# Graph aggregation of a four-layer graph network in 64x64 tiles of the PE array, with re-paired batches and two output banks

## The chip, the cores and the metric

The kernel runs on one core of one Trainium2 chip. The metric is the device time of that core in microseconds (us); less is better. Of the kernel before there are three timed runs: 1529.56, 1530.80 and 1532.76 us, median 1530.8 us.

## The reference, cut to what matters

A batch of 128 graphs, each with 64 nodes and 256 features in fp32, passes through four residual layers that share one 64x64 adjacency matrix. Layers 0 and 1 are masked multi-head attention, layer 2 is graph attention, and layer 3 is a gated recurrence of three steps. The change touches layer 2 alone:

```
h = maximum(layernorm(x), 0)          # [128, 64, 256]
hw = h @ W                            # [128, 64, 256]
e = leaky_relu(hw @ a1 [:, :, None] + hw @ a2 [:, None, :], 0.2) * adj
att = softmax(e, axis=2)              # [128, 64, 64], one matrix for each graph
x = x + elu(att @ hw + beta * hw)
```

So `att @ hw` is, for each of 128 graphs, a product of a 64x64 matrix with a 64x256 matrix.

## The kernel before, in words

**Tiling.** `x` stays in SBUF for the whole run, as 64 tiles of 128 partitions by 256 features. A tile holds two graphs, one on partitions 0 to 63 and one on 64 to 127. Work goes in chunks of `CT` = 4 tiles (eight graphs), so there are 16 chunks. PSUM is eight banks: four are named `scores` (in the later part also `high`), four `ring`.

**Stages.** Layers 0 and 1 run as one pipeline over 32 chunk steps and take about the first 600 us. Then comes a stage in which layers 2 and 3 are interleaved: `halves` issues 49 half steps of the recurrence, six for a group of two chunks, and layer 2 of the next group's chunks is put between them. Each half step has attributes that say what it carries. Where `graph_a` is set (half steps 1 and 3 of a group), TensorE transposes the normalised rows of a chunk (`graph_rows`, line 1536) and multiplies them by `W` (`graph_product`); ScalarE copies the result into `hw`; `graph_s2` makes the second score term. Where `graph_b` is set (half steps 2 and 4), TensorE transposes the attention matrices (`graph_attT`), VectorE adds beta times the identity and writes `attT` (`copy_attT`), and TensorE makes the aggregation (`graph_aggregate`, line 1558). Layer 2 of chunks 0 and 1 runs ahead of that: chunk 0's aggregation in the last steps of layer 1, into `scores`; chunk 1's in `begin`, into `ring`, from `hw_next`.

**The aggregation before.** `attT[:, t, :]` is a 128x128 block-diagonal matrix with the transposed attention of the two graphs of tile `t`. It is the stationary operand; the moving operand is `hw[:, t, 0:256]`. One matmul for each tile, four for a chunk, each shown in the trace as two instructions (fp32 goes through the array twice). Tiles 0 and 1 fill bank `bank`, tiles 2 and 3 bank `bank + 1`; after two tiles `y_ready` goes up.

**Who reads it.** ScalarE reads each bank once (`graph_read`, line 805: minus the negative part, into `y_neg`), then takes an exponential (line 810). VectorE adds the positive part of each bank to `x` (`graph_positive`, line 1199) and then the exponential (line 1210). In a half step that carries an aggregation TensorE's order is: eight transposes, `u3` (12 matmuls of 512 columns), `adjacency` (line 1579), `u5` (12), transposes of the attention (line 1556), `w4` (12), the aggregation, `w3` (12), `w5` (12). These products all go through the helper at line 99. VectorE's order is r_sum (1249), the low parts (1301), z_sum (1254, two instructions), `graph_positive` (1199), 1210, then of the next half step r times h (1273) and `rhp_lo` (1275), for which `u5` waits.

**Matmuls in 64x64 tiles that are there already.** `adjacency` issues 32 matmuls with 64 rows, 64 output partitions and 64 moving columns, in the order of the four quarters of the array: input rows of half `g` go to bank `g`, output partitions of half `c`. All take `adjT` as moving operand. `graph_s2` issues eight matmuls that alternate between two diagonal quarters. `values` of layers 0 and 1 (line 1448) uses tiles of 64 rows by 32 output columns, eight of them in turn, each with a moving operand of its own.

**Order and waits.** Every engine's program is written out by hand in order; semaphores are the only links. Where the count waited for is a register (inside a hardware loop), the helper `wait_apart` (line 34) first waits for at least one and then for the count.

Of the kernel before, what the change touches and what calls it, by code (L numbers as in the profile page):

```python
# [11 lines left out]
B, N, D = 128, 64, 256  # L12
HEADS = 8
HD = D // HEADS
P = 128
# [3 lines left out]
CT = 4  # L19
CW = CT * P  # L20
CHUNKS = TILES // CT
FT = D // P
# [5 lines left out]
def wait(eng, sem, count):  # L28

    if not isinstance(count, int) or count > 0:  # L30
        eng.wait_ge(sem, count)


def wait_apart(eng, sem, count):


    if not isinstance(count, int):
        eng.wait_ge(sem, 1)
    eng.wait_ge(sem, count)
# [78 lines left out]
def network(nc, x, ident, psum, layers, a, out):  # L118
# [9 lines left out]
    with Phase(nc) as ctx:  # L128
        plan = Plan(nc)

        def sb(name, shape, dt=F32, at=None):
            return plan.put(name, shape, dt, at)

        def sem(name):
            return ctx.semaphore(nc, name)
# [47 lines left out]
        start = plan.starts  # L183
# [6 lines left out]
        y_neg = w_stage[:, 0, :, :].rearrange("p o (c d) -> p (o c) d", d=D)  # L190
# [8 lines left out]
        attT = sb("attT", [P, CT, P], F32, at_w1 + 8224)  # L199
        beta_ident = sb("beta_ident", [P, P], F32, at_w1 + 10272)  # L200
        adjT = sb("adjT", [P, P], F32, at_w1 + 10784)
        g_hn = sb("g_hn", [P, CT, D], F32, start["hn"])
# [108 lines left out]
        g_xT_ready = sem("g_xT_ready")  # L311
# [15 lines left out]
        attT_copied = sem("attT_copied")  # L327
        y_ready = sem("y_ready")
# [121 lines left out]
        def rows_of(c, t, width):  # L450
            return x[:, bass.ds(c * CT + t, width), :]
# [5 lines left out]
        with nc.Block() as block:  # L457
# [198 lines left out]
            def _(act):  # L656
# [144 lines left out]
                def graph_read(c, psum=ring, bank=2):  # L801
                    wait(act, g_x_done, c)
                    for g in range(2):
                        act.wait_ge(y_ready, c * 2 + g + 1)
                        act.activation(y_neg[:, 2 * g:2 * g + 2, :], psum[:, bank + g, :].rearrange("p (t c) -> p t c", t=2),
                                       ACT.Relu, scale=-1.0).then_inc(y_read, 1)

                def graph_exp(c):
# [3 lines left out]
                def graph_out(c, psum=ring, bank=2):  # L812
                    graph_read(c, psum, bank)
                    graph_exp(c)
# [7 lines left out]
                def begin(s):  # L822
                    for m in range(FT):
                        act.wait_ge(hu_ready, m + 1)
                        act.activation(hu[:, m, :], ring[:, 2 + m, :], ACT.Copy).then_inc(hu_copied, 1)
                    graph_read(1, ring, 0)
                    agg_high(0)
                    graph_exp(1)
                    o_normalise(T + 1, 1, 1)
                    o_normalise(T + 2, 0, 1)  # L830
                    act.wait_ge(b_ready, 5)
                    r_tanh(0)
                    norm_rows(rn, r_hn[1], 1, 1)
                    enter(1, 1)
                    graph_normalise(2, 0)
# [108 lines left out]
            def _(dve):  # L944
# [250 lines left out]
                def graph_positive(c, psum=ring, bank=2):  # L1195
                    for g in range(2):
                        dve.wait_ge(y_read, c * 2 + g + 1)
                        xc = rows_of(c, 2 * g, 2)
                        dve.scalar_tensor_tensor(xc, psum[:, bank + g, :].rearrange("p (t c) -> p t c", t=2), 0.0, xc,
                                                 ALU.max, ALU.add).then_inc(x_plus_pos, 1)  # L1200

                def graph_out(c, psum=ring, bank=2):
                    graph_positive(c, psum, bank)
                    graph_negative(c)
# [51 lines left out]
                def begin(s):  # L1256
                    graph_positive(1, ring, 0)
                    agg_low(0)
                    graph_negative(1)
                    recurrence_stats(1)  # L1260
                    r_sum(0)
                    z_sum(0)
                    rows_stats(gn, 2)
                    final_sum(T + 2, 0, 1)
                    enter(1, 1)
# [91 lines left out]
            def _(pe):  # L1357
# [170 lines left out]
                def transposes(rows, psum, bank, signal):  # L1528
                    for f in range(FT):
                        for t in range(CT):  # L1530
                            last = pe.transpose(psum[:, bank + f, t * P:(t + 1) * P], rows[:, t, f * P:(f + 1) * P],  # L1531
                                                ident[:])
                        last.then_inc(signal, 1)

                def graph_rows(c, psum=ring):
                    pe.wait_ge(gn.hn_ready, c + 1)
                    transposes(g_hn, psum, 0, g_xT_ready)

                def graph_product(c, t, psum=ring, bank=2):
                    stat = [pair(g_hT, slice(None), k, slice(t * P, (t + 1) * P)) for k in range(FT)]  # L1540
# [17 lines left out]
                    last.then_inc(attT_ready, 1)  # L1558

                def graph_aggregate(c, psum=ring, bank=2, src=hw):  # L1560
                    pe.wait_ge(attT_copied, c + 1)
                    for g in range(2):
                        for t in (2 * g, 2 * g + 1):
                            last = pe.matmul(psum[:, bank + g, (t % 2) * D:(t % 2 + 1) * D], attT[:, t, :],  # L1564
                                             src[:, t, 0:D], start=True, stop=True)
                        last.then_inc(y_ready, 1)

                def enter(c, q, psum=ring):
                    pe.wait_ge(rn.hn_ready, c + 1)
# [15 lines left out]
                def begin(s):  # L1585
                    pe.wait_ge(h0_lo_ready, FT)
                    pe.wait_ge(x_done, T * 2)
                    for m in range(FT):
                        product(pe, ring[:, 2 + m, :], columns(wT["u3"], m), moving(hp[0])).then_inc(hu_ready, 1)
                    graph_aggregate(1, ring, 0, hw_next)  # L1590
                    pe.wait_ge(e_sum, 2)
                    pe.wait_ge(hw_copied, 2 * FT)
                    pe.wait_ge(adj_loaded, 32)
                    adjacency(r_hn[0])
                    pe.wait_ge(agg_lo_ready, FT)
                    pe.wait_ge(x_plus_pos, 4)
                    for m in range(FT):
                        product(pe, ring[:, m, :], columns(wT["w4"], m), moving(agg)).then_inc(r_ready, 1)
                    for m in range(FT):
                        product(pe, high[:, m, :], columns(wT["w3"], m), moving(agg)).then_inc(z_ready, 1)  # L1600
                    for m in range(FT):
                        product(pe, high[:, 2 + m, :], columns(wT["w5"], m), moving(agg), ends=False)
                    pe.wait_ge(hu_copied, FT)
                    enter(1, 1)

                def half(s):
# [4 lines left out]
                    if not s.last:  # L1611
# [30 lines left out]
                        if s.graph_a is not None:  # L1642
                            if s.step == 0:
                                pe.wait_ge(r_added, n * FT)
                            graph_rows(s.graph_a)
# [26 lines left out]
                    if s.graph_b is not None:  # L1672
                        graph_aggregate(s.graph_b)
# [28 lines left out]
                o_half(T - 1, 1, 0)  # L1702
                pe.wait_ge(s_masked, (T - 1) * R + 2)
                graph_rows(0, high)
                o_half(T - 1, 1, 1)
                values(T - 1, 1)
# [6 lines left out]
                graph_s2(0, high, 2)  # L1713
                p_transposes(T, 0)
                graph_rows(1, high)
                o_products(T, 1)
                values(T, 0)
                graph_attT(0, high, 2)
                pe.wait_ge(g_hT_lo_ready, 2 * FT)
                graph_product(1, 0, high, 0)  # L1720
                graph_product(1, 1, high, 0)
                graph_aggregate(0, high, 2)
                pe.wait_ge(hw_copied, FT + 1)
                graph_product(1, 2, high, 0)
# [65 lines left out]
```

## Time and profile before

| what | value |
|---|---|
| median of three runs | 1530.8 us |
| the profiled execution's own time | 1531.08 us |
| its span, first to last instruction | 1529.3 us |
| mean granted TensorE clock, of full speed | 0.987 |
| VectorE busy | 1245.6 us |
| ScalarE busy | 991.0 us |
| GpSimd busy | 534.7 us |

The profiled execution takes 1.8 us more than its span, for what lies around the first and the last instruction, and 0.3 us more than the median. TensorE's matmuls are pipelined and their records overlap: a record is as long as one matmul takes from start to end, so the pitch between starts, not the record's length, tells how long the array is taken.

### The profile page before, as it was taken

The numbers are of one execution on the slowest core, as the hardware profiler recorded it, in microseconds if no ns is written. First come the engines' busy times: TensorE is split into PE (matmuls) and PEld (weight loads), VectorE is DVE, ScalarE is ACT, GpSimd is POOL, SyncE is SP. The second block draws the span as 40 slices with busy tenths as digits, with TensorE's granted clock in tenths as the row PEclk, the third lists the DMA queues.
The fourth block names the chain that finished last, engine by engine and source line by source line (L and its number), as shares of the span: only waits on it lengthen the run. The fifth ranks groups of instructions, "written<-read, shape, count | busy, mean of one in ns | idle before, by whom it ended". The sixth has DMA issues, their size and how long they took to land.

```text
span 1529.3 us, 45415 instructions
## 1 busy us (share of the span) xinstructions
PE 1471.4 (96%) x18712; PEld 1250.6 (82%) x18712; DVE 1245.6 (81%) x2510; ACT 991.0 (65%) x1792; POOL 534.7 (35%) x622
## 2 busy tenths in 40 slices
PE   5899999899999998799999999999999999999997
PEld 4889989799898887688888888888888888888885
DVE  4777887988899999788888888888888888888675
ACT  4766677677777776666666666666666666666553
POOL 2676767566788886411111101101111111111000
PEclk9999999999999999899999999999999999999998
DMA  8200000002322334100000000000000000000000
GB/s 263 85 3 0 0 0 1 16 16 44 57 55 57 70 66 58 29 1 1 29 1 1 29 1 1 29 1 1 29 1 1 29 1 1 29 1 1 29 1 28
DMA packets 36822, 40.88 MB, mean 27 GB/s; under 512 B 11856, under 2 KB 31824, under 8 KB 36688
## 3 DMA queue, kind: packets, MB, share of 16 engines
q0 software_dynamic: 4608, 16.78, 5.8%
q1 hardware_dynamic: 32080, 22.10, 4.8%
q8 instruction: 110, 1.80, 0.5%
q14 instruction: 24, 0.20, 0.0%
HBM read 13.71 MB, written 8.39 MB: 14 GB/s over the span
## 4 chain that ended last, share of the span: by engine, by line
PE 80%; DVE 10%; POOL 4%; issue 3%; ACT 2%; DMA 0%; POOLq 0%; DVEq 0%; ACTq 0%
PE ring L99 36%; PE scores L99 27%; PE scores L1579 3%; PE ring L1408 2%; PE scores L1372 2%; PE ring L1619 2%; PE ring L1564 2%; DVE total L993 2%; PE ring L1448 2%; PE ring L1531 2%; POOL s L534 1%; PE ring L1419 1%; POOL rstd L525 1%; DVE stats L965 1%; PE ring L1691 1%
## 5 line engine op out<-in xcount | busy, mean ns | idle before, releaser
L534 POOL TENSOR_TENSOR s<-s,mx 128x512 f32<-128x512 f32 x128 | 137.4, 1092 | 48.0 <-DVE mx L989 48.0
L540 POOL TENSOR_TENSOR s<-s,rtotal 128x512 f32<-128x512 f32 x128 | 131.4, 1065 | 34.1 <-DVE rtotal L995 33.9
L600 POOL TENSOR_TENSOR r_var_eps<-r_mean_var,eps 128x4 f32<-128x4 f32 x16 | 8.1, 509 | 384.6 <-DVE r_mean_var L1146 384.6
L684 ACT ACTIVATE s<-s 128x512 f32<-128x512 f32 x128 | 78.3, 644 | 75.4 <-POOL s L534 75.1
L1275 DVE TENSOR_TENSOR rhp_lo<-r,rhp_hi 128x1024 fp32r<-128x1024 f32 x48 | 58.8, 1225 | 72.7 <-ACT rhp_hi L865 72.7
L984 DVE SCALAR_TENSOR_TENSOR s<-scores,mask 128x512 f32<-128x512 f32 x128 | 87.1, 681 | 33.9 <-PE scores L1372 33.9
L884 ACT ACTIVATE hv<-scores,bias 128x512 f32<-128x512 f32 x96 | 66.1, 688 | 59.7 <-PE scores L99 59.7
L858 ACT ACTIVATE later_w<-ring 128x512 f32<-128x512 f32 x64 | 34.7, 595 | 107.2 <-PE ring L1619 107.2
L847 ACT ACTIVATE r<-r,bias_half 128x512 f32<-128x512 f32 x96 | 64.4, 717 | 59.6 <-DVE r L1249 59.6
L696 ACT ACTIVATE pT<-ring 128x512 f32<-128x512 f32 x128 | 66.0, 603 | 45.4 <-PE ring L1408 45.4
L989 DVE TENSOR_REDUCE mx<-s 128x8 f32<-128x512 f32 x128 | 87.9, 686 | 4.4
L1240 DVE TENSOR_TENSOR agg_lo<-scores,agg_hi 128x512 fp32r<-128x512 f32 x96 | 61.8, 685 | 33.3 <-ACT agg_hi L840 32.8
L99 PE MATMUL scores<-rhp_hi,u5T_hi 128*128 128x512 f32 x192 | 81.4, 424 | 1.8 <-DVE rhp_lo L1275 1.8
L993 DVE TENSOR_REDUCE total<-s 128x8 f32<-128x512 f32 x128 | 82.6, 645 | 0.0
L99 PE MATMUL ring<-agg_hi,w4T_hi 128*128 128x512 f32 x192 | 78.9, 411 | 2.0 <-DVE agg_lo L1240 2.0
L99 PE MATMUL scores<-agg_hi,w5T_hi 128*128 128x512 f32 x192 | 78.7, 410 | 0.0
L99 PE MATMUL scores<-agg_hi,w3T_hi 128*128 128x512 f32 x192 | 78.3, 408 | 0.0
L1254 DVE TENSOR_TENSOR later_w<-scores,hu 128x512 f32<-128x512 f32 x96 | 64.3, 685 | 15.4 <-PE scores L99 15.4
L99 PE MATMUL scores<-rhp_lo,u5T_hi 128*128 128x512 f32 x192 | 76.6, 399 | 0.0
L99 PE MATMUL scores<-rhp_hi,u5T_lo 128*128 128x512 f32 x192 | 76.5, 399 | 0.0
L99 PE MATMUL ring<-agg_lo,w4T_hi 128*128 128x512 f32 x192 | 76.3, 398 | 0.0
L99 PE MATMUL ring<-agg_hi,w4T_lo 128*128 128x512 f32 x192 | 76.3, 397 | 0.0
(288 smaller groups left out, 5077.7 us busy)
## 6 DMA issues: line engine op xcount, KB each, us to landing
x<-beta_less_one POOLq DMA_DIRECT2D x16, 512.0 KB, 4.7
x<-o POOLq DMA_DIRECT2D x16, 512.0 KB, 6.6
out_x<-x SPq DMA_DIRECT2D x16, 512.0 KB, 3.2
x<-in_x SPq DMA_DIRECT2D x1, 6144.0 KB, 25.3
later_w<-in_L_gnn_w_w SPq DMA_DIRECT2D x3, 512.0 KB, 6.0
x<-in_x SPq DMA_DIRECT2D x2, 512.0 KB, 5.3
x<-in_x SPq DMA_DIRECT2D x1, 1024.0 KB, 8.0
stage<-in_L_gnn_w_qkv SPq DMA_DIRECT2D x3, 256.0 KB, 3.0
```

Source lines behind the costliest of these rows:

```text
L99: last = pe.matmul(out, s, m, start=(begins and n == 0), stop=(ends and n == len(terms) - 1))
L534: pool.tensor_tensor(sr, sr, mx[:, r, :].unsqueeze(2).to_broadcast([P, CT * 2, N]), ALU.subtract).then_inc(s_shifted, 1)
L540: pool.tensor_tensor(sr, sr, rtotal[:, r, :].unsqueeze(2).to_broadcast([P, CT * 2, N]), ALU.mult).then_inc(p_ready, 1)
L684: act.activation(s[:, par, r, :, :, :], s[:, par, r, :, :, :], ACT.Exp).then_inc(p_exp, 1)
L696: act.activation(pT[:, r, :, :].rearrange("p t q -> p (t q)"), ring[:, r, :], ACT.Copy).then_inc(pT_copied, 1)
L847: act.activation(r[:, m, :], r[:, m, :], ACT.Tanh, bias=bias_half[:, 1, m:m + 1], scale=0.5)\
L884: act.activation(hv[:, m, :], high[:, 2 + m, :], ACT.Tanh, bias=bias[:, 2, m:m + 1])\
L984: dve.scalar_tensor_tensor(sr(par, r), scores[:, r, :].rearrange("p (a k) -> p a k", k=N), SCALE, masks[layer_of(i, lay)][:].unsqueeze(1). ...
L989: dve.reduce_max(mx[:, r, :], sr(par, r), AX.X).then_inc(s_max, 1)
L993: dve.reduce_sum(total[:, r, :], sr(par, r), AX.X).then_inc(p_total, 1)
L1240: dve.tensor_tensor(agg.lo[:].rearrange("p m (t g q) -> p g m t q", t=CT, g=2)[:, g], high[:, g, :].rearrange("p (m t q) -> p m t q", m=FT ...
L1254: dve.tensor_tensor(z[:, m, :], high[:, m, :], hu[:, m, :], ALU.add).then_inc(z_added, 1)
```

## The change

The aggregation is issued as eight matmuls of 64 rows by 64 output partitions for a chunk, each with one graph's attention block as stationary operand and 256 moving columns. The order goes through the four quarters of the array: first tiles 0 and 1 of the chunk (`a` = 0), then tiles 2 and 3. The row half `g` from which a matmul reads decides its bank, so the two banks hold the upper and the lower row groups' results. Both `y_ready` signals now come in the last set of four. The wait for `attT_copied` uses `wait_apart`.

So that every graph's result lands on its own partitions of `x`, the graphs 0, 1, 2, 3 of a pair of tiles are placed differently in `hw`: its even tile holds graphs 0 and 3, its odd tile 1 and 2. `graph_rows` does that by writing the transposes' two 64-column parts to separate places of the bank, for odd tiles in descending order. ScalarE and VectorE, which read one bank at a time, now write and read tiles `g` and `g + 2` of the chunk where they had two neighbouring tiles. The number and size of their instructions stay.

```diff
@@ ScalarE, graph_read
-                        act.activation(y_neg[:, 2 * g:2 * g + 2, :], psum[:, bank + g, :].rearrange("p (t c) -> p t c", t=2),
+                        act.activation(y_neg[:, g:CT:2, :], psum[:, bank + g, :].rearrange("p (t c) -> p t c", t=2),
                                        ACT.Relu, scale=-1.0).then_inc(y_read, 1)
@@ VectorE, graph_positive
-                        xc = rows_of(c, 2 * g, 2)
+                        xc = rows_of(c, 0, CT)[:, g:CT:2, :]
@@ TensorE, graph_rows
                     pe.wait_ge(gn.hn_ready, c + 1)
-                    transposes(g_hn, psum, 0, g_xT_ready)
+                    for f in range(FT):
+                        four = psum[:, f, :].rearrange("p (a b n) -> p a b n", a=CT // 2, n=N)
+                        for t in range(CT):
+                            places = four[:, t // 2, 0:4:2, :] if t % 2 == 0 else four[:, t // 2, 3:0:-2, :]
+                            last = pe.transpose(places, g_hn[:, t, f * P:(f + 1) * P], ident[:])
+                        last.then_inc(g_xT_ready, 1)
@@ TensorE, graph_aggregate
-                    pe.wait_ge(attT_copied, c + 1)
-                    for g in range(2):
-                        for t in (2 * g, 2 * g + 1):
-                            last = pe.matmul(psum[:, bank + g, (t % 2) * D:(t % 2 + 1) * D], attT[:, t, :],
-                                             src[:, t, 0:D], start=True, stop=True)
-                        last.then_inc(y_ready, 1)
+                    wait_apart(pe, attT_copied, c + 1)
+                    for a in range(2):
+                        for g in range(2):
+                            own = slice(g * N, (g + 1) * N)
+                            for to in range(2):
+                                t = 2 * a + (g + to) % 2
+                                last = pe.matmul(psum[to * N:(to + 1) * N, bank + g, a * D:(a + 1) * D],
+                                                 attT[own, t, own], src[own, t, 0:D], start=True, stop=True)
+                            if a == 1:
+                                last.then_inc(y_ready, 1)
```

## Rows read from the trace of the kernel before

**Rows 1.** The page: busy time of TensorE, and the chain that ended last.

```profile
PE 1471.4 (96%) x18712; PEld 1250.6 (82%) x18712; DVE 1245.6 (81%) x2510; ACT 991.0 (65%) x1792; POOL 534.7 (35%) x622
PE 80%; DVE 10%; POOL 4%; issue 3%; ACT 2%; DMA 0%; POOLq 0%; DVEq 0%; ACTq 0%
```

**Rows 2.** TensorE in 200 us stretches: length, busy (instructions), granted clock, DMA.

```profile
600.00:800.00 200.00, 188.75 (x1518) 0.96 0.06 14
...
1000.00:1200.00 200.00, 199.79 (x1662) 1.00 0.03 9
1200.00:1400.00 200.00, 199.61 (x1623) 1.00 0.03 9
```

**Rows 3.** All of TensorE's waits from 660 to 1400 us: total, times, longest.

```profile
PE ring L99 <- issue: 1.7, 4, 0.7
```

**Rows 4.** Timeline of TensorE around one aggregation: start, length in us, what.

```profile
938.93 0.39 PE L99 MATMUL ring<-agg_hi,w4T_lo 128*128 128x512 f32 x1
939.16 1.89 PE L1564 MATMUL ring<-hw,attT 128*128 128x256 f32 x8
940.70 0.58 PE L99 MATMUL scores<-agg_hi,w3T_hi 128*128 128x512 f32 x1
941.12 0.40 PE L99 MATMUL scores<-agg_lo,w3T_hi 128*128 128x512 f32 x1
941.35 0.39 PE L99 MATMUL scores<-agg_hi,w3T_lo 128*128 128x512 f32 x1
```

**Rows 5.** Instruction groups by line and shape: count, busy us, mean ns.

```profile
L1564 PE MATMUL ring<-hw,attT 128*128 128x256 f32 x112 | 26.4, 378 | 0.0
L1531 PE MATMUL ring<-ident,g_hn 128*128 128x128 f32 x112 | 14.5, 272 | 0.0
```

**Rows 6.** Timeline of TensorE around one `adjacency`.

```profile
949.70 0.39 PE L99 MATMUL ring<-hp_b_lo,u3T_hi 128*128 128x512 f32 x1
949.93 0.40 PE L99 MATMUL ring<-hp_b_hi,u3T_lo 128*128 128x512 f32 x1
950.26 1.16 PE L1579 MATMUL scores<-adjT,later_w 64*64 64x64 f32 x64
951.35 0.50 PE L99 MATMUL scores<-rhp_hi,u5T_hi 128*128 128x512 f32 x1
951.69 0.40 PE L99 MATMUL scores<-rhp_lo,u5T_hi 128*128 128x512 f32 x1
```

**Rows 7.** Timeline of TensorE around one `graph_s2`.

```profile
924.37 0.39 PE L99 MATMUL scores<-agg_hi,w3T_lo 128*128 128x512 f32 x1
924.69 0.68 PE L1548 MATMUL ring<-ident,hw 64*64 64x64 f32 x16
...
925.65 0.39 PE L99 MATMUL scores<-agg_lo,w5T_hi 128*128 128x512 f32 x1
```

**Rows 8.** Line 1448 (`values`) in its first 0.27 us: instructions in brackets.

```profile
86.30:86.57 0.27, 0.26 (x32) 1.00 0.22 61
```

**Rows 9.** Timeline of VectorE behind the aggregation of rows 4.

```profile
942.77 0.68 DVE L1254 TENSOR_TENSOR later_w<-scores,hu 128x512 f32<-128x512 f32 x1
943.88 0.69 DVE L1254 TENSOR_TENSOR later_w<-scores,hu 128x512 f32<-128x512 f32 x1 [0.43 <-PE scores L99]
...
949.29 1.22 DVE L1275 TENSOR_TENSOR rhp_lo<-r,rhp_hi 128x1024 fp32r<-128x1024 f32 x1 [1.12 <-ACT rhp_hi L865]
```

**Rows 10.** Timeline of all engines around the aggregation in `begin`.

```profile
624.67 1.89 PE L1564 MATMUL ring<-hw_next,attT 128*128 128x256 f32 x8
...
626.42 1.50 DVE L1199 SCALAR_TENSOR_TENSOR x<-ring,x 128x512 f32<-128x512 f32 x2 [1.45 <-ACT later_w L805]
626.49 1.16 PE L1579 MATMUL scores<-adjT,r_hn_a 64*64 64x64 f32 x64
...
628.32 1.29 DVE L1240 TENSOR_TENSOR agg_lo<-scores,agg_hi 128x512 fp32r<-128x512 f32 x2 [0.40 <-ACT agg_hi L840]
...
629.66 0.50 PE L99 MATMUL ring<-agg_hi,w4T_hi 128*128 128x512 f32 x1 [2.01 <-DVE agg_lo L1240]
```

**Rows 11.** Timeline of ScalarE behind chunk 0's aggregation.

```profile
606.29 0.60 ACT L805 ACTIVATE later_w<-scores 128x512 f32<-128x512 f32 x1 [1.32 <-PE scores L1564]
607.35 0.60 ACT L805 ACTIVATE later_w<-scores 128x512 f32<-128x512 f32 x1 [0.46 <-PE scores L1564]
```

## The prediction

> **What bounds the kernel now.** I read the page first: TensorE is busy for 96% of the span and holds 80% of the chain that ended last [rows 1]. Then TensorE by stretches: from 1000 to 1400 us it is busy for 399.4 of 400 us at a granted clock of 1.00 [rows 2]. Then its waits from 660 to 1400 us: 1.7 us in 740 [rows 3]. Fourteen of the 16 aggregations lie in that part (112 instructions, eight for a chunk [rows 5]); the other two lie in the stage from 600 to 660 us, where the engine does wait. So in the steady part the program ends sooner by exactly the array time that is taken out, as long as no other engine's result then comes too late.
>
> **What the old block costs.** The last `w4` starts at 938.93 and the aggregation at 939.16, the pitch of the 512-column products. Behind it the first `w3` record (940.70, 0.58 long) is queued early; the second starts at 941.12, the third at 941.35, so the pitch is 0.23 and the first one got the array at 941.12 - 0.23 = 940.89. The block holds the array for 940.89 - 939.16 = 1.73 us, eight instructions at 0.215 [rows 4].
>
> **What the new block costs.** Sixteen instructions of 256 moving columns in quarter tiles. I need the number of quarters that run together, the time of a round, and the cost of going from whole-array to quarter tiles and back.
>
> Together: `adjacency` starts 64 instructions of 64 columns in a record of 1.16 us [rows 6]. A 256-column instruction holds the array for 0.215 [rows 4], so 64 columns want a quarter of that, 0.054, and 64 of them one after another 3.4 us. They run four at a time.
>
> Going in and out: `adjacency` runs from 950.26 to 951.69 - 0.23 = 951.46, 1.20 us for 16 rounds of four [rows 6]; `graph_s2` from 924.69 to 925.65 - 0.23 = 925.42, 0.73 us for eight rounds of two [rows 7]. The difference of eight rounds is 0.47, so a round is 0.059 and the fixed part is 1.20 - 16 x 0.059 = 0.26. Ahead of the block the gap from the last whole-array product is 950.26 - 949.93 = 0.33 in place of 0.23, 0.10 more; before `graph_s2` it is 0.32, the same. Fixed cost together 0.35 us, in both.
>
> Sum: 16 instructions / 4 = 4 rounds of 0.215, 0.86, plus 0.35 = 1.21 us. Saved for a chunk 1.73 - 1.21 = 0.52, for 14 chunks **7.2 us**. The bounds are from the same rows: a round could be as much dearer as it is in `adjacency` (0.059 for 0.054, +0.005 each, 0.02 for a chunk); if all 16 went one by one the block would be 3.4 + 0.35, if two by two 8 x 0.215 + 0.35 = 2.07. I take four, because the order of the quarters and the split of banks by row half are those of `adjacency`. What differs is that `adjacency` has one moving operand for all, while here the two column halves of a row half stream different columns. The nearest row for that is `values`: eight tiles, each fed by its own operand, 32 instructions of 64 columns within 0.27 us, where one by one they would want 1.7 [rows 8]. Six or more run together there, with four different streams on the same rows.
>
> A rule of the Trainium skill speaks against a part of this. The fixed part of 0.26 contains the weight loads that nothing covers in the first round, and every later round of `adjacency` fits into 0.059, so its loads, 64 columns each, are covered by the round before on the same rows [rows 6]. The page "TensorE: Matmul & The Clock Gate", section "Part 3: Packing small matmuls — row/col tiling", says that a weight load overlaps matmuls in flight only when its row group differs; elsewhere the page allows it for a background buffer too. By the strict rule the loads of rounds two to four would be bare, the trace speaks against it, and what it would give is a rival below. The page "TensorEngine Tiling (Array Packing)", section "Key Properties", says that changing the tiling mode drains the engine; the 0.35 us of rows 6 and 7 is that price here, and by leaving it out the gain would be 0.87 for a chunk.
>
> **The other edits.** *Transposes.* 128 instructions (16 chunks of eight) keep their size; only the places written differ. No row of the trace has TensorE writing parts 64 columns apart or in descending order. They hold the array for 14.5 / 112 = 0.13 us each at most, by the busy time [rows 5]; below, nothing reason offers makes a scattered write faster, so the bounds are 0 and, if the write took twice as long, +0.11 to 0.13 each, +14 to 17 us for 128. I take 0: what paces a transpose is the stream of 128 columns, and every other output goes out column by column in any case. *ScalarE and VectorE.* The same sizes in two pieces of 256 elements; each piece is as long as before, so 0, within +-0.05 us for each of 64 instructions off TensorE's path. *The added wait instruction* in the loop: queued behind it are the weight loads of the aggregation. TensorE's sequencer is ahead of the array there by the queued `w4` products, which cover it; without that cover it would cost its own 0.05 us, ten times, 0.5. *The first bank's signal.* It now comes with the second: before, at half of 1.73, plus one record; now at about 1.05 plus one record. 0.15 us later for the first bank, 0.5 earlier for the second. In rows 9 VectorE comes to 1199 only after z_sum, so neither matters.
>
> **What is late next.** Behind the block, z_sum's second instruction waits 0.43 us for `w3` (943.88); the first ends at 942.77 + 0.68 = 943.45. With `w3` 0.52 earlier the second starts at 943.45 or so: 0.43 of the 0.52 is passed on, and VectorE is then the limit by 0.09. Its chain ends in `rhp_lo` at 949.29 + 1.22 = 950.51 [rows 9], and `u5` starts at 951.35 [rows 6]: 0.84 spare, of which 0.09 goes. The saving reaches the array whole.
>
> **The two blocks outside.** In `begin` the block is followed by `adjacency`, so there is no way back to whole-array tiles: 624.67 + 0.10 + 0.05 for the first bare load + 0.86 = 625.68, where `adjacency` began streaming at 626.54. That is 0.86 earlier. But VectorE has two instructions of 1199 (from 626.42, each 0.6 apart) ahead of `agg_lo`; with the two reads starting near 625.85 these start at about 626.47, end at 627.67, and `agg_lo` can start then in place of 628.32 [rows 10]. The `w4` that waits for it comes 0.65 earlier. Chunk 0's block runs at a lower clock (539 ns mean record against 378). Its two readers start at 606.29 and 607.35 [rows 11]; the 1.06 between them is half the block at that clock. With four rounds in place of eight the block is about 0.6 shorter and both signals come near 606.7, so the second read starts one read's pitch later, about 607.25: 0.1 earlier. Together **0.75**.
>
> Sum: 7.2 + 0.75 = 7.95 off the profiled execution's 1531.08, 1523.1; the median stands 0.3 below that execution, so **1522.9 us**, 0.5% faster.
>
> **The rivals.**
> *A: bare weight loads.* In `adjacency` the first round's load costs about 0.05 more than a covered one (64 columns at 0.215 / 256 each are 0.054). If rounds two to four each paid it, a block costs 0.16 more and 14 save 5.0: 1525.1. Against it: the 0.059 rounds. It is the mechanism of the page's row-group rule.
> *B: the two column halves take turns*, because each row half has to feed two different 256-column streams. Then a block is 2.07, 0.34 more than before: 14 x 0.34 = +4.8, plus some 0.5 outside: 1536. It decides at 1.73 - 0.35 = 1.38, that is 6.4 rounds of 0.215: with more than that the kernel is slower. For it: `adjacency` shares one operand. Against it: rows 8. Wholly one by one it would be 1531 + 14 x 2.0 = 1559.
> *C: the saving becomes waits.* The array gets to each dependency 0.5 sooner, and a chain that I have not followed is short by that. The smallest spare I see is the 0.84 above less 0.09; if each of the 14 gave its saving back, only the 0.75 outside would be left, 1530.
> *D: scattered transposes* cost over 0.06 us more each: the 7.95 is gone at 7.95 / 128 = 0.062, half their present array time. No row speaks for it or against it. At double: 1537.
> *E: the clock.* From 600 to 800 us the granted clock was 0.96 [rows 2], so some 16 of these 200 us ran at 1.2 GHz (0.04 x 200 / 0.5), in the stage where the engine waits. Shifted events can move, add or drop a part of them; I allow a tenth to a fifth, +-1.5 us; this widens every case and is none of its own.
>
> **How the numbers follow.** Forecast 0.74 (own range 1520.5 to 1524.5), A 0.09, B 0.06, C 0.07, D 0.04. A change under 0.2%, 3.1 us, can't be told from none here. Forecast and A are faster, and some of D and C: 0.85. Same: most of C and a small D, 0.07. Slower: B and half of D, 0.08. The range takes the forecast, A, and C's nearer part: 1520 to 1528.5.
>
> **What would show it.** Right: the block's record about 1.2 us with `w3`'s virtual start (second start less 0.23) 1.21 behind it, still four starts to each 0.215 to 0.22; z_sum's wait of 0.43 gone; TensorE's waits from 660 to 1400 still under 3 us; transposes at the same 272 ns and pitch. A shows as rounds of 0.27; B as pairs 0.215 apart; C as new waits of `u5`, `w4` or `u3`; D as transposes over 0.11 apart. The prediction is wrong if the block costs over 1.5 us, or if it costs 1.2 and the time stays within 3 us.

## The result, and the profile after

| | before | after |
|---|---|---|
| median | 1531.99 us (20 runs) | 1523.45 us (20 runs) |
| range of the runs | 1528.47 to 1537.72 | 1520.55 to 1528.16 |
| the profiled execution | 1531.08 us | 1525.95 us |
| its span | 1529.3 us | 1524.2 us |

The ratio after to before is 0.9945, with a 95% interval of 0.9935 to 0.9955: 8.5 us less, where 7.95 was forecast. In time that is 1523.45 us, where 1522.9 was forecast from a median before of 1530.8, which over 20 runs is 1531.99. The two profiled executions are only 5.1 us apart, since that of before lies 0.9 under its median and that of after 2.5 over its own. So the gain is best read between marks of the trace.

The page of after, beside [rows 1]. TensorE has 128 more instructions (eight for each of 16 chunks) and is 7.7 us less busy; VectorE and ScalarE are as before, within 1 us:

```profile
PE 1463.7 (96%) x18840; PEld 1233.9 (81%) x18840; DVE 1244.6 (82%) x2510; ACT 991.5 (65%) x1792; POOL 534.8 (35%) x622
```

TensorE by stretches, beside [rows 2]. It is still full in the steady part, and from 600 to 800 us somewhat more of the time was at the half clock (0.95 for 0.96):

```profile
600.00:800.00 200.00, 186.53 (x1650) 0.95 0.08 17
1000.00:1200.00 200.00, 199.51 (x1702) 1.00 0.03 9
1200.00:1395.00 195.00, 194.75 (x1642) 1.00 0.03 9
```

Its waits from 655 to 1395 us, beside [rows 3]. A freed dependency did not turn into a wait:

```profile
PE ring L99 <- issue: 1.4, 4, 0.5
```

The block, beside [rows 4]; it is the aggregation of the same chunk:

```profile
939.76 0.40 PE L99 MATMUL ring<-agg_hi,w4T_lo 128*128 128x512 f32 x1
940.09 1.09 PE L1573 MATMUL ring<-hw,attT 64*64 64x256 f32 x16
941.12 0.50 PE L99 MATMUL scores<-agg_hi,w3T_hi 128*128 128x512 f32 x1
941.45 0.40 PE L99 MATMUL scores<-agg_lo,w3T_hi 128*128 128x512 f32 x1
941.68 0.39 PE L99 MATMUL scores<-agg_hi,w3T_lo 128*128 128x512 f32 x1
```

Read as the old one was: `w3` got the array at 941.45 - 0.23 = 941.22, the block began at 940.09, and the gap ahead of it is 0.33 in place of 0.23. So 1.13 + 0.10 = 1.23 us, where 1.73 stood and 1.21 was forecast. Each of the 14 blocks reads the same.

All instructions of the aggregation in the steady part. First of before, then of after: duration min/median/max in ns, first and last start in us.

```profile
L1564 PE MATMUL ring<-hw,attT x112: 377/378/379, 675.6 to 1390.7; 128*128 128x256 f32 x112
```

```profile
L1573 PE MATMUL ring<-hw,attT x224: 373/376/427, 679.1 to 1386.3; 64*64 64x256 f32 x112
```

A quarter-tile matmul lasts as long as a whole-array one; there are twice as many, and four run at a time. The first start is 3.5 us later in the changed kernel and the last 4.4 earlier, so 7.9 us were won in between. Of these 0.8 come from the last block's own shape (its last start is 1.5 us behind its first in before, 0.7 in after), and 7.1 from the 13 blocks ahead of it with what lies between them.

The 3.5 us that the changed kernel was behind at 679 had other causes. It was 3.7 behind at 580 us already, before any changed instruction had run: the starts of the same TensorE instructions lie 0.2 us apart near 85, 0.7 near 91 and 3.6 at 410 us. Of the 3 us between 388 and 410, half comes from a stretch at half clock (1.2 GHz) that only the profile of after has there: from 392 to 396 us the granted clock is 1.00 in before and 0.57 in after. The other half are two pauses of TensorE in `values` that are longer in after by 0.5 and 0.9 us (the first is 2.08 us for 1.53, ahead of that stretch); why they are longer stays open. That is what makes the two profiled executions an unlucky pair.

`begin`, beside [rows 10]. ScalarE now makes both reads (805) and then `agg_hi` without a pause, and VectorE's `agg_lo` follows right behind its two instructions of 1199:

```profile
628.36 0.39 PE L99 MATMUL ring<-hp_a_hi,u3T_lo 128*128 128x512 f32 x1
...
628.68 1.09 PE L1573 MATMUL ring<-hw_next,attT 64*64 64x256 f32 x16
...
629.60 1.11 PE L1589 MATMUL scores<-adjT,r_hn_a 64*64 64x64 f32 x64
629.87 1.08 ACT L805 ACTIVATE later_w<-ring 128x512 f32<-128x512 f32 x2 [0.48 <-PE ring L1573]
630.50 1.29 DVE L1199 SCALAR_TENSOR_TENSOR x<-ring,x 128x512 f32<-128x512 f32 x2 [1.65 <-ACT later_w L805]
630.84 1.09 ACT L840 ACTIVATE agg_hi<-scores 128x512 fp32r<-128x512 f32 x2
631.70 1.28 DVE L1240 TENSOR_TENSOR agg_lo<-scores,agg_hi 128x512 fp32r<-128x512 f32 x2
...
633.04 0.50 PE L99 MATMUL ring<-agg_hi,w4T_hi 128*128 128x512 f32 x1 [2.33 <-DVE agg_lo L1240]
```

In before the last product ahead of the block is this one:

```profile
624.44 0.40 PE L99 MATMUL ring<-hp_a_hi,u3T_lo 128*128 128x512 f32 x1
```

From the start of that product to `adjacency` 1.24 us, where it was 2.05; to `w4` 4.68, where it was 5.22: 0.81 and 0.54 less. Counted from the aggregation's own start it would be 0.90 and 0.63, but that leaves out the gap ahead of the block, which grew from 0.23 to 0.32.

VectorE behind the block, beside [rows 9]. The wait of 0.43 us before z_sum's second instruction is gone; the two now run back to back:

```profile
943.60 1.31 DVE L1254 TENSOR_TENSOR later_w<-scores,hu 128x512 f32<-128x512 f32 x2
...
949.63 1.23 DVE L1275 TENSOR_TENSOR rhp_lo<-r,rhp_hi 128x1024 fp32r<-128x1024 f32 x1 [1.13 <-ACT rhp_hi L865]
```

`rhp_lo` ends at 950.86, `u5` starts at 951.67, so 0.81 us are spare, where 0.84 were.

### The profile page after: what moved, and what is told of

The parts are those of the page before. It is cut to its first block, busy times and chain, and to the rows that moved or that the text cites. A ratio compares the mean times of both kernels' runs of the same rounds, so it can differ in the third digit from the quotient of the medians.

```text
span 1524.2 us, 45691 instructions
## 1 busy us (share of the span) xinstructions
PE 1463.7 (96%) x18840; PEld 1233.9 (81%) x18840; DVE 1244.6 (82%) x2510; ACT 991.5 (65%) x1792; POOL 534.8 (35%) x622
## 4 chain that ended last, share of the span: by engine, by line
PE 87%; DVE 7%; POOL 2%; ACT 2%; issue 2%; DMA 0%; DVEq 0%; POOLq 0%; ACTq 0%
PE ring L99 40%; PE scores L99 27%; PE scores L1589 3%; PE ring L1408 3%; PE scores L1372 2%; PE ring L1448 2%; PE ring L1629 2%; PE ring L1419 1%; PE ring L1573 1%; PE ring L1701 1%; PE ring L1531 1%; POOL s L534 1%; PE ring L1542 1%; DVE total L993 1%; DVE stats L955 1%
## 5 line engine op out<-in xcount | busy, mean ns | idle before, releaser
L600 POOL TENSOR_TENSOR g_var_eps<-g_mean_var,eps 128x4 f32<-128x4 f32 x16 | 8.2, 513 | 193.1 <-DVE g_mean_var L1146 193.1
```

## The experiments

### Only the transposes changed

```diff
 # the kernel before, and in graph_rows:
-                    transposes(g_hn, psum, 0, g_xT_ready)
+                    ... the changed kernel's loop, with `places`
```

> The kernel before with the changed graph_rows alone: the 128 transposes of layer 2 write their 64-column parts to scattered places, in descending order for odd tiles; the aggregation is the old one with four whole-array matmuls. hw then pairs the graphs otherwise than the aggregation and x assume, so layer 2's sums go to other graphs. Theory (a scattered write costs the array nothing): 1.000 of before, and a pitch of 0.109 us between transposes as before. Rival (a scattered write is slower, and the whole change gained in spite of it): at double time +14 us, ratio 1.009; the changed kernel's records of these transposes are 277 ns in the mean against 272, and if those 5 ns each were array time it would be 128 x 0.005 = 0.6 us, ratio 1.0004, which only the pitch can tell from nothing.

Measured: 1532.70 us, ratio 1.000 (0.9987 to 1.0012). The group of these transposes, then one of its timeline with what follows:

```profile
L1542 PE MATMUL ring<-ident,g_hn 128*128 128x128 f32 x112 | 14.5, 272 | 0.0
```

```profile
801.91 1.04 PE L1542 MATMUL ring<-ident,g_hn 128*128 128x128 f32 x8
802.88 0.64 PE L1585 MATMUL scores<-adjT,later_w 64*64 64x64 f32 x28
```

One such group of before:

```profile
911.20 1.04 PE L1531 MATMUL ring<-ident,g_hn 128*128 128x128 f32 x8
912.17 0.34 PE L1579 MATMUL scores<-adjT,later_w 64*64 64x64 f32 x8
```

Mean 272 ns [rows 5] and 0.97 us from the first transpose to the quarter tiles, both as before; from start to start they stand 0.109 us apart in both. Writing 64-column parts to scattered places, also in descending order, costs the array nothing. Rival D falls. The 277 ns of the changed kernel are not this edit's: here the edit is alone and the mean is 272. There they come from one group of eight, of which the first three and part of the fourth ran at half clock; the granted clock around it was 0.64:

```profile
650.65 1.42 PE L1542 MATMUL ring<-ident,g_hn 128*128 128x128 f32 x8
```

```profile
650.50:651.80 1.30, 1.30 (x8) 0.64 0.00 0
```

Its first three steps from start to start are 0.21 us, and the group takes 0.38 us more than one of before. The 104 transposes behind it have the mean of 272 ns and the pitch of 0.109 again.

### Two quarters at a time

```diff
 # the kernel before, with
+                    ... the wait for attT_copied by wait_apart
+                    for t in range(CT):
+                        for g in range(2):
+                            own = slice(g * N, (g + 1) * N)
+                            last = pe.matmul(psum[own, bank + t // 2, (t % 2) * D:(t % 2 + 1) * D],
+                                             attT[own, t, own], src[own, t, 0:D], start=True, stop=True)
+                    ... y_ready goes up behind every second t
```

> The kernel before with the aggregation as eight 64x64 matmuls on the two diagonal quarters of the array only, in the old layout, one bank for two tiles; no re-pairing. Theory (the gain is made by four quarters at a time, and a change of tile size costs 0.35 us): rounds of two, 8 x 0.215 + 0.35 = 2.07 us for a block in place of 1.72, so 14 x 0.35 = +4.9 us, some 5.5 with the two outer blocks, ratio 1.003 to 1.004. Rival (less data in each matmul is what makes it faster): a ratio under 0.998.

Measured: 1535.84 us, ratio 1.0021 (1.0006 to 1.0036).

```profile
678.75 0.40 PE L99 MATMUL ring<-agg_hi,w4T_lo 128*128 128x512 f32 x1
679.07 1.95 PE L1565 MATMUL ring<-hw,attT 64*64 64x256 f32 x16
680.95 0.50 PE L99 MATMUL scores<-agg_hi,w3T_hi 128*128 128x512 f32 x1
681.28 0.40 PE L99 MATMUL scores<-agg_lo,w3T_hi 128*128 128x512 f32 x1
```

The block is 681.28 - 0.23 - 679.07 + 0.09 = 2.07 us, as expected. By the ratio the kernel is 3.2 us slower, where 4.9 to 5.5 was expected; the interval, 0.9 to 5.5 us, just takes that in. Small tiles alone don't make the kernel faster; it is the re-pairing, which lets all four quarters work, that gains. It also shows that the two row halves may write one bank together as long as they write different partitions: the rounds stand 0.216 apart. In the changed kernel they write the same partitions, and there each has a bank of its own; whether one bank would do for both wasn't tried.

### Each aggregation in two blocks

```diff
 # the changed kernel, where graph_aggregate takes only the values of a that parts names, and in half:
-                        graph_aggregate(s.graph_b)
+                        graph_aggregate(s.graph_b, parts=(0,))
                     if not s.last:
                         for m in range(FT):
                             product(pe, high[:, m, :], columns(wT["w3"], m), moving(agg)).then_inc(z_ready, 1)
+                            if m == 0 and s.graph_b is not None:
+                                graph_aggregate(s.graph_b, parts=(1,))
```

> The changed kernel with each of the 14 aggregations of the steady part cut in two blocks, tiles 0 and 1 ahead of w3's first six products and tiles 2 and 3 behind them. Theory (going into 64x64 tiles and back costs 0.35 us each time): each block 0.43 + 0.35 = 0.78 us, together 1.56 for 1.21, so 14 x 0.35 = +4.9 us over the changed kernel, about 0.9945 + 0.0032 = 0.9977 of before. Rival (most of the 0.35 lies in the unequal lengths of the products beside it, not in the change of tiles): under +0.15 us a block, +2 us, ratio 0.9958 or less.

Measured: 1529.74 us, ratio 0.9981 (0.9968 to 0.9993). The first of the two blocks:

```profile
715.03 0.40 PE L99 MATMUL ring<-agg_hi,w4T_lo 128*128 128x512 f32 x1
715.35 0.66 PE L1574 MATMUL ring<-hw,attT 64*64 64x256 f32 x8
715.95 0.50 PE L99 MATMUL scores<-agg_hi,w3T_hi 128*128 128x512 f32 x1
716.28 0.39 PE L99 MATMUL scores<-agg_lo,w3T_hi 128*128 128x512 f32 x1
```

716.28 - 0.23 - 715.35 + 0.09 = 0.79. The second starts at 717.53, 0.32 behind the product ahead of it, and is as long to 0.01 us: 1.57 or 1.58 together, 0.35 or 0.36 over the undivided block. By the ratios the kernel is 5.5 us slower than the changed one, where 4.9 was expected. So the way into quarter tiles and back costs some 0.36 us each time it is gone. Both blocks have the same neighbours as the whole one, so the split alone doesn't tell the change of tiles from unequal lengths of neighbouring products. The old block does: eight whole-array instructions of 256 columns among the same products took 1.73 us, and 8 x 0.215 is 1.72 [rows 4]. Unequal lengths without a change of tiles cost 0.01.

### The same matmuls, quarter by quarter

```diff
-                    for a in range(2):
-                        for g in range(2):
-                            for to in range(2):
+                    for g in range(2):
+                        for to in range(2):
+                            for a in range(2):
+                    ... y_ready goes up once for each g
```

> The changed kernel with the same eight matmuls in another order: both matmuls of one quarter of the array directly after each other, then the next quarter. Theory (TensorE starts its instructions in program order, so neighbours in the program must be in different quarters to run together): of 16 instructions only the last of one quarter and the first of the next overlap, 13 rounds of 0.215 + 0.35 = 3.1 us a block in place of 1.21, 14 x 1.9 = +27 us, ratio 1.012 of before. Rival (each quarter has a queue of its own, and order does not matter): the block stays at 1.21 us and the ratio at 0.9945.

Measured: 1526.95 us, ratio 0.996 (0.9941 to 0.9978). The theory fell. Besides the order, `y_ready` now goes up once behind each row half's four matmuls.

```profile
713.86 0.40 PE L99 MATMUL ring<-agg_hi,w4T_lo 128*128 128x512 f32 x1
714.18 1.11 PE L1573 MATMUL ring<-hw,attT 64*64 64x256 f32 x16
715.23 0.50 PE L99 MATMUL scores<-agg_hi,w3T_hi 128*128 128x512 f32 x1
715.56 0.40 PE L99 MATMUL scores<-agg_lo,w3T_hi 128*128 128x512 f32 x1
```

The block is 715.56 - 0.23 - 714.18 + 0.09 = 1.24 us, 0.01 to 0.02 over the changed kernel's. What the order changes is the step between the starts in a round. Windows on this line alone, first of this kernel and then of the changed one, from the block's first start (matmuls in the first brackets, weight loads in the second):

```profile
714.18:714.24 0.06, 0.06 (x4) 0.06 (x5) 1.00 0.00 0
714.25:714.44 0.19, 0.19 (x4) 0.16 (x8) 1.00 0.00 0
```

```profile
940.09:940.12 0.03, 0.03 (x4) 0.03 (x4) 1.00 0.00 0
940.13:940.33 0.20, 0.20 (x4) 0.17 (x8) 1.00 0.00 0
```

Four start within 0.06 us (steps of 0.014) where the changed kernel has them within 0.03 (steps of 0.007), and then no more for the length of a round. The records don't name the quarter. But with two quarters in use the rounds were of two instructions (the diagonal kernel), so a quarter takes one at a time, and four that start within 0.06 us belong to four quarters, though each quarter's four instructions stand together in the program. A quarter whose next instruction is not yet due does not hold up the others. That each has a queue of its own is one way to read it; no run here shows how it is done.

### Every aggregation issued twice

```diff
-                    for a in range(2):
+                    for turn, a in enumerate((0, 1, 0, 1)):
...
-                            if a == 1:
+                            if turn == 3:
```

> The changed kernel with every aggregation's eight matmuls issued twice, to the same places. Theory (a round of four costs 0.215 us and the fixed part 0.35 once for a block; TensorE is the bound): a block is 8 x 0.215 + 0.35 = 2.07 us, +0.86, with 14 blocks +12.0 and about 1.5 for the other two: 13.5 us over the changed kernel, ratio 0.9945 + 0.0088 = 1.003. Rival (rounds of 256 columns are cheaper than 0.215, and the 1.21 is mostly the fixed part): under +8 us.

Measured: 1537.79 us, ratio 1.0028 (1.0015 to 1.004).

```profile
720.43 0.40 PE L99 MATMUL ring<-agg_hi,w4T_lo 128*128 128x512 f32 x1
720.75 1.96 PE L1573 MATMUL ring<-hw,attT 64*64 64x256 f32 x32
722.64 0.50 PE L99 MATMUL scores<-agg_hi,w3T_hi 128*128 128x512 f32 x1
722.98 0.40 PE L99 MATMUL scores<-agg_lo,w3T_hi 128*128 128x512 f32 x1
```

722.98 - 0.23 - 720.75 + 0.09 = 2.09 us, 0.86 more for four more rounds. By the ratios the kernel is 12.7 us slower than the changed one, where 13.5 was expected.

### Half of every aggregation left out

```diff
-                    for a in range(2):
+                    for a in range(1):
...
-                            if a == 1:
+                            if a == 0:
```

> The changed kernel with only the first four matmuls of each aggregation (tiles 0 and 1 of the chunk); tiles 2 and 3 are left out, so half of layer 2's aggregation is missing. Theory (TensorE stays the bound beyond the change): 0.43 us less for a block, 14 x 0.43 = -6.0 and some -0.5 outside, ratio 0.9945 - 0.0042 = 0.990. Rival (with the changed kernel VectorE's z_sum or another chain is already the limit, which then keeps the time up): less than -3 us, ratio over 0.9925, and new waits of TensorE between 660 and 1390 us.

Measured: 1517.47 us, ratio 0.9891 (0.9871 to 0.9911). TensorE's waits from 680 to 1390 us, all of them:

```profile
PE ring L99 <- issue: 2.5, 4, 0.7
```

The block:

```profile
713.50 0.40 PE L99 MATMUL ring<-agg_hi,w4T_lo 128*128 128x512 f32 x1
713.83 0.66 PE L1573 MATMUL ring<-hw,attT 64*64 64x256 f32 x8
...
714.75 0.39 PE L99 MATMUL scores<-agg_lo,w3T_hi 128*128 128x512 f32 x1
```

It takes 714.75 - 0.23 - 713.83 + 0.10 = 0.79 us, 0.43 less than the changed kernel's. By the ratios the kernel is 8.3 us faster than the changed one, where 6.5 was expected, with an interval of some 3 us on each side. TensorE is still the bound. But in the two profiles not all of it is won, as all the aggregation's starts in the steady part show:

```profile
L1573 PE MATMUL ring<-hw,attT x112: 376/402/427, 675.8 to 1379.2; 64*64 64x256 f32 x112
```

From the first block's start to the last block's it is 703.1 us (675.8 to 1378.9), where the changed kernel has 706.5 (679.1 to 1385.6): 3.4 us less, and 13 x 0.43 would be 5.6. Of the missing 2.2 us, 1.1 are in the four waits above (2.5 for 1.4 us), which are 1.4 to 2.5 us in all these kernels. Another 0.8 are something new: once in each group of two chunks, the transposes of `h_a` start 0.37 us behind the last product of `w3`, where in the changed kernel (738.27, 738.50) they start 0.23 behind it.

```profile
734.13 0.40 PE L99 MATMUL scores<-agg_hi,w3T_lo 128*128 128x512 f32 x1
734.50 1.06 PE L1701 MATMUL ring<-ident,h_a 128*128 128x128 f32 x8
```

That is 0.13 to 0.14 us, six times. The list of waits misses it, since the record of the product ahead still covers the pause. What the transposes wait for isn't shown, but it is a path with little time to spare that the prediction had not found. So the changed kernel shows nothing of rival C, but a step further it begins.

Together the kernels with quarter rounds of four give a line: 2 rounds 0.79 us, 4 rounds 1.22 or 1.23, 8 rounds 2.09. That is about 0.216 for a round and 0.36 fixed.

## Why the prediction was right

- *The bound.* TensorE is full in the steady part before and after, and time put into its block goes to the end, as far as the ratios tell: +3.2 us for the diagonal where 14 x 0.35 = 4.9 stand in the trace (interval +0.9 to +5.5), +12.7 for twice where 14 x 0.86 = 12.0 do. The 0.50 us that the change takes out arrive too. Of a further 0.43 some 0.06 a block turn into a new wait (0.8 us for 13).
- *Four at a time.* 0.215 for a round of 256 columns. B, the column halves taking turns, falls: twice four quarters in 0.86 more, with different operands on the same rows.
- *The fixed part.* Forecast 0.35 from `adjacency` and `graph_s2`, measured 0.36, by itself in the split. The words "in both" were no check: two blocks had been solved for two unknowns, a round and a fixed part, on the assumption that a round of two lasts as long as a round of four. The assumption holds (0.216 in the diagonal kernel), and the line through three lengths is the check.
- *Four different streams.* `values` was read too high. Of the 32 instructions begun in its first 0.27 us the last ones had hardly streamed. The whole block is 128 instructions in 1.49 us, where one by one they would want 6.9: between four and five at a time, not six or more.

```profile
86.31 1.49 PE L1448 MATMUL ring<-pT,v 64*32 64x64 f32 x128
```

  Four at a time is all that the forecast needed, and this row still speaks for it.
- *Weight loads.* From 940.38 to 940.55, within the second round of the changed kernel's block (windows on this line alone: matmuls in the first brackets, among them the records of the round before that still run; weight loads in the second), the next round's four loads run beside the matmuls, on the same rows:

```profile
940.38:940.55 0.17, 0.17 (x8) 0.13 (x4) 1.00 0.00 0
```

  The rounds start 0.216 apart but for the second, which comes 0.05 later because only the first round's loads are bare. A, bare loads in every round, falls. The rule of the Trainium skill (page "TensorE: Matmul & The Clock Gate", section "Part 3: Packing small matmuls — row/col tiling") that a load overlaps only with matmuls of another row group does not hold in this stream; the page's exception for a background buffer would fit it. That the engine drains at a change of mode (the Trainium skill, page "TensorEngine Tiling (Array Packing)", section "Key Properties") agrees with the fixed 0.36 us; the runs show the price, not the draining.
- *The block.* 1.73 to 1.22 or 1.23, 0.50 to 0.51 saved, forecast 0.52. That is 7.0 us for 14 blocks, forecast 7.2. The 7.1 us between the marks for 13 blocks are 0.6 more than 13 x 0.50; 0.3 of these are the four waits of rows 3, which vary from 1.4 to 2.5 us between these profiles; the rest isn't traced.
- *The transposes.* Taken at 0 between bounds of 0 and 17 us; the experiment gives 0, within 2 us by its interval and within 1 ns each by the pitch. The step that counted, that a scattered write costs nothing, was an assumption with no row behind it, and it came true.
- *`begin`.* Forecast 0.86 to `adjacency` and 0.65 to `w4`, measured 0.81 and 0.54.
- *z_sum.* The wait of 0.43 is gone as forecast, and VectorE has become its limit; 0.03 of the spare time went, where 0.09 was forecast.
- *Chunk 0's block.* Forecast 0.1 earlier. Here this can't be told: the changed kernel was 3.7 us behind ahead of the block (at 580) and 3.7 behind after it (606.96 and 610.62 are the next product's starts), but in between its start stood 4.5 behind, since the products ahead of it ran longer at half clock. The block itself held the array for 1.83 us (608.79 to 610.62), where it was 2.62 (604.34 to 606.96). No gain in time shown, none excluded at this size.
- *The clock.* Taken at 0 +-1.5 us. Behind the last block, where nothing was changed, the changed kernel's profile wins another 1.0 us: `u5` near the end ran in part at half clock in before (0.72 granted from 1513 to 1519 us) and at the full clock in after (1.00 from 1509 to 1515). Such stretches move each pair of executions by an amount like that.

What is left open is small: the blocks give 7.0 us and `begin` 0.5, together 7.5. The 8.5 us of the medians are 1.0 more, and the interval of the ratio (0.9935 to 0.9955, or 6.9 to 10.0 us) takes in both. Each part that could be measured was forecast a little too large, and the difference to the medians isn't traced to any part; that 7.95 lies between the two is not to be read as finer agreement than that.

## What to carry to other kernels

A product of block-diagonal matrices fills half of a stationary operand with zeros. It pays to split it only if the four quarters of the array all get work at once, and that can need a new pairing of the data, which here was free because transposes write wherever they are told. Each stay in quarter tiles costs a fixed 0.36 us beside whole-array products, so a block must save more than that: here 8 whole rounds against 4 quarter rounds do, while 8 rounds of two do not. And a sum made from two other blocks of the same kernel, of unequal length, gives the fixed part and the round before anything is built.

## What was not expected of the hardware

The order of the matmuls among the quarters hardly matters: two for one quarter right behind each other cost 0.01 to 0.02 us for a block, where 1.9 had been expected from starts in strict program order. Matmuls of the two row halves write one bank at the same time without loss if they write different partitions (0.216 a round in the diagonal kernel).
